# A post-norm decoder layer: P x V in two products per block, stacking by head, the last norm on VectorE, new orders

## The reference

```
Q, K = (x @ Wq.T + bq, x @ Wk.T + bk) in 16 heads of 32, each times 32**-0.25
V = x @ Wv.T + bv
x = norm(x + softmax(causal(Q K^T)) V @ Wo.T + bo)
q, k = ctx @ Wq2.T + bq2, ctx @ Wk2.T + bk2          # ctx 4 x 512 x 256, width 128
A = softmax(q k^T);  x = norm(x + x @ A^T)
xq = quantise(rms(x)), 127 steps of the row's maximum
x = norm(x + (silu(xq @ sign(Wg).T) * (xq @ sign(Wu).T)) @ sign(Wd).T)   # hidden 2048
```

## Time and profile before

| | |
|---|---|
| time, median of 3 runs (lowest, highest) | 658.28 us (655.01, 659.70) |
| the profiled execution | 660.73 us, its span 659.0 us |
| busy: TensorE, VectorE, ScalarE, GpSimd | 630.6, 496.5, 412.6, 340.8 us |
| mean granted TensorE clock | 0.983 of full speed |
| moved | 45.70 MB, 69 GB/s over the span |

### The profile page before, as it was taken

How to read it: one execution, slowest core, us unless ns; L and a number is a source line. 1 busy time by engine, 2 the same in 40 slices (tenths; PEclk the granted TensorE clock), 3 DMA queues, 4 the chain that set the end, 5 groups by cost and what they waited for, 6 DMA issues and landing times.

```text
span 659.0 us, 15461 instructions
## 1 busy us (share of the span) xinstructions
PE 630.6 (96%) x6156; PEld 445.1 (68%) x6156; DVE 496.5 (75%) x1006; ACT 412.6 (63%) x759; POOL 340.8 (52%) x472
## 2 busy tenths in 40 slices
PE   6896899999999999999999999999999999999996
PEld 5583477777666676667866766676867766586563
DVE  5764677869978977749859987866966996888764
ACT  5665799954647896434466697653456586593342
POOL 8302588514749744325477753614537743563452
PEclk9896889999999999999999999999999999999999
DMA  9696441452011011023213101031111200001000
GB/s 320 190 267 167 150 157 40 170 178 49 12 39 67 2 34 35 25 89 81 50 27 88 34 2 34 12 78 42 38 45 45 71 1 1 1 19 48 1 33 32
DMA packets 31463, 45.70 MB, mean 69 GB/s; under 512 B 5664, under 2 KB 22560, under 8 KB 29856
## 3 DMA queue, kind: packets, MB, share of 16 engines
q1 hardware_dynamic: 30848, 44.20, 22.7%
q10 hardware_dynamic: 544, 0.52, 0.2%
HBM read 27.79 MB, written 4.19 MB: 49 GB/s over the span
## 4 chain that ended last, share of the span: by engine, by line
PE 78%; DVE 10%; ACT 4%; DMA 3%; issue 3%; SPq 1%; POOL 0%; POOLq 0%; DVEq 0%; ACTq 0%
PE ps_b L657 28%; PE ps_b L840 16%; PE ps_b L825 13%; PE ps_b L752 6%; PE ps_b L733 5%; PE ps_b L761 3%; PE ps_b L714 2%; PE ps_b L710 2%; DMA hp<-in_sgT_dram 2%; PE ps_b L716 2%; DVE negm L1091 1%; SPq L619 1%; PE ps_b L670 1%; DVE bn L1027 1%; DMA st<-mrow 1%
## 5 line engine op out<-in xcount | busy, mean ns | idle before, releaser
L1284 POOL TENSOR_TENSOR ph<-p,ph 128x512 f16<-128x512 f32 x96 | 109.8, 1158 | 31.6 <-ACT ph L858 31.4
L825 PE MATMUL ps_b<-xqT,sg 128*128 128x256 f16 x1024 | 125.4, 272 | 0.1
L1280 POOL TENSOR_TENSOR hp<-gt,hp 128x512 f16<-128x512 f32 x64 | 73.9, 1160 | 87.2 <-ACT hp L858 87.0
L840 PE MATMUL ps_b<-sd,hp 128*128 128x512 fp8e4 x512 | 118.2, 379 | 0.2 <-DVE qk L1076 0.2
L1091 DVE TENSOR_REDUCE negm<-ps_b 128x1 f32<-128x512 f32 (+3 forms) x176 | 103.2, 632 | 18.4 <-PE ps_b L716 18.2
L825 PEld LDWEIGHTS ps_b<-xqT,sg 128*128 128x128 fp8e4 x1024 | 97.9, 98 | 16.6 <-DVE negm L1091 0.5
L1242 POOL TENSOR_SCALAR_AFFINE_SELECT p<-p 128x256 f32<-128x256 f32 (+1 forms) x96 | 45.7, 486 | 77.8 <-ACT p L920 76.9
L657 PE MATMUL ps_b<-xhl,wh 128*128 128x256 f16 x480 | 83.7, 273 | 0.2
L840 PEld LDWEIGHTS ps_b<-sd,hp 128*128 128x128 f16 x512 | 49.0, 98 | 51.4 <-DVE qk L1076 0.3
L1004 ACT ACTIVATE gt<-gt 128x512 f32<-128x512 f32 x64 | 40.0, 633 | 47.2 <-DVE gt L1198 47.1
L920 ACT ACTIVATE p<-ps_b 128x512 f32<-128x512 f32 x96 | 55.4, 605 | 21.5 <-PE ps_b L733 21.1
(11 more groups left out here) (133 smaller groups left out, 1218.9 us busy)
## 6 DMA issues: line engine op xcount, KB each, us to landing
st<-qk SPq DMA_DIRECT2D x192, 64.0 KB, 2.0
hp<-in_sgT_dram SPq DMA_DIRECT2D x6, 1024.0 KB, 7.1
gt<-in_sgT_dram SPq DMA_DIRECT2D x6, 1024.0 KB, 5.7
rows<-in_x_dram SPq DMA_DIRECT2D x8, 512.0 KB, 3.7
out_dram<-rows SPq DMA_DIRECT2D x16, 256.0 KB, 2.1
xin<-in_xT_dram SPq DMA_DIRECT2D x14, 256.0 KB, 3.7
e<-in_ctxT_dram SPq DMA_DIRECT2D x4, 512.0 KB, 5.6
hp<-in_wT_dram SPq DMA_DIRECT2D x4, 256.0 KB, 4.6
```

Source lines behind the costliest of these rows:

```text
L825: ins = pe.matmul(ps[:, a * HALF:(a + 1) * HALF], sg[:, ("gg", "uu").index(name), c, ht * P:(ht + 1) * P], xqT[:, c, :], start=c == 0, sto ...
L840: ins = pe.matmul(ps[:, :], hp[:, (UNITS * s + n) % HP_SLOTS, h, a, t * P:(t + 1) * P], sd[:, ht, :], start=ht == h == 0, stop=ht == HT - ...
L1280: pool.tensor_tensor(slot[:, 1, :, :], tg[:, n % 2, :, :], slot[:, 0, :, :], ALU.subtract)\
L1284: pool.tensor_tensor(out_, in_, hi, ALU.subtract).then_inc(signal, 1)
```

## The change

Four parts. (1) `weigh`: high P times [high values, ones, low values] is one product of 65 columns, low P times [high values, ones] a second of 33. Each slot of a group has 65 columns of the bank in place of 33; the eighth (t = 1, j = 3) would begin at 455 and pass column 512, so it keeps three products in 33 columns. A new step on ScalarE (`low_products`, word ov in its order) copies the low products of the seven other slots into o, and `divide` on VectorE adds them to the high ones in PSUM before reciprocal and division. o has a new layout for it. (2) A stack is now four steps of three transfers, one for each head, with a semaphore each; a maximum product waits only for the heads that it reads. (3) The norms of the last two tiles (zn3.1.0, zn3.1.1) run on VectorE; the other 14 stay on ScalarE. (4) All five orders are new texts.

```diff
--- before.py
+++ after.py
...
-lw0.0 lw0.1 lw0.2 lw0.3 lw1.0 lw1.1 lw1.2 lw1.3 lw2.0 lw2.1 lw2.2 lw2.3 lx0.1 lc0 bi lw3 sm sk0.0.0 lg0 sk0.0.1 lx1.0
...
+lw0.0 lw0.1 lw0.2 lw0.3 bi lw1.0 lw1.1 lw1.2 lw1.3 lc0 lw2.0 lw2.1 lw2.2 lw2.3 lx0.1 lg0 sm lw3 lg1 sk0.0.0.0 lg2
...
@@ -398,7 +407,7 @@
         p32 = sb("p32", [P, P32_SLOTS, S], F32)
         ph = sb("ph", [P, PH_SLOTS, 2, S], F16)
         osum = sb("osum", [P, 2, 2 * HG], F32)
-        o = sb("o", [P, T, D], F32)
+        o = sb("o", [P, 2, NG, 2, P], F32)
         rows = sb("rows", [P, T, D], F32)
         scaled = sb("scaled", [P, D], F32)
         xq = sb("xq", [P, 2, D], F16)
@@ -458,7 +467,7 @@
         r_in = [Signal(f"r_in{h}", 16) for h in range(2)]
         x_hi, x_lo = Signal("x_hi", 2), Signal("x_lo", 2)
         qk_hi, qk_lo = Signal("qk_hi", 2 * NG), Signal("qk_lo", 2 * NG)
-        stacked = [Signal(f"stacked{i}", 12 * 16) for i in range(2)]
+        stacked = [[Signal(f"stacked{i}_{j}", 3 * 16) for j in range(HG)] for i in range(2)]
         v_hi, v_lo = Signal("v_hi", 2), Signal("v_lo", 2)
         bm_red = Signal("bm_red", 1)
         m_hi, m_lo = Signal("m_hi", 2), Signal("m_lo", 2)
@@ -466,6 +475,7 @@
         p_exp, p_mask, p_hi, p_lo = Signal("p_exp", 1), Signal("p_mask", 1), Signal("p_hi", 1), Signal("p_lo", 1)
         q_exp, q_lo = Signal("q_exp", 1), Signal("q_lo", 1)
         pv_done = Signal("pv_done", NG * HG)
+        o_low, o_add = Signal("o_low", NG), Signal("o_add", NG)
         o_sum, o_out = Signal("o_sum", NG), Signal("o_out", NG)
         c_hi, c_lo = Signal("c_hi", CC), Signal("c_lo", CC)
         cq_hi, cq_lo = Signal("cq_hi", 2), Signal("cq_lo", 2)
@@ -538,6 +548,11 @@
             where = place_of(n)
             return p_lo if has_diagonal(where[0], where[2]) else q_lo, 0, among(*where) + 1
 
+        def blocks_of(ps, first, blocks, width):
+
+            whole = ps[:, :]
+            return bass.AP(whole.tensor, whole.offset + first, [whole.ap[0], [VW, blocks], [1, width]])
+
         def ph_free(eng, n):
 
             if n >= PH_SLOTS:
@@ -604,7 +619,8 @@
                 half = x[b].rearrange("(t p) d -> p t d", p=P)[:, 2 * h:2 * h + 2, :]
                 sp.dma_start(rows[:, 2 * h:2 * h + 2, :], half).then_inc(r_in[h].sem, 16)
 
-            def stack(s, gp):
+            def stack(s, gp, j):
+
                 b, h = divmod(s, 2)
                 n = 2 * s + gp
                 if n >= Q_SLOTS:
@@ -615,10 +631,9 @@
                 wait(sp, qk_lo, s, 4 * gp + 4)
                 q, k = n % Q_SLOTS, Q_SLOTS + 2 * gp + h
                 for r, (first, step) in enumerate(((0, 2), (1, 1), (0, 3))):
-                    for j in range(HG):
-                        sp.dma_start(st[DH * r:DH * (r + 1), q:k + 1:k - q, j, :, :],
-                                     qk[DH * j:DH * (j + 1), gp, first:first + step + 1:step, :, :])\
-                          .then_inc(stacked[gp].sem, 16)
+                    sp.dma_start(st[DH * r:DH * (r + 1), q:k + 1:k - q, j, :, :],
+                                 qk[DH * j:DH * (j + 1), gp, first:first + step + 1:step, :, :])\
+                      .then_inc(stacked[gp][j].sem, 16)
 
             def shift_rows(s, gp):
                 wait(sp, m_lo, s, gp + 1)
@@ -701,7 +716,8 @@
             def score_max(s, g, k):
                 h, gp, task = s % 2, g // 2, ("mx", s, g, k)
                 wait_for(pe, consts, CONSTS)
-                wait(pe, stacked[gp], s, 12 * 16)
+                for j, _, _ in MX_PIECES[h][k]:
+                    wait(pe, stacked[gp][j], s, 3 * 16)
                 ps = open_bank(task)
                 for j, qt, col in MX_PIECES[h][k]:
                     q = st[0:3 * DH, (2 * s + gp) % Q_SLOTS, j, g % 2, qt % 2 * P:(qt % 2 + 1) * P]
@@ -742,36 +758,38 @@
                     open_bank(task)
                 ps = psum[place[task][0]]
                 for t in range(2):
-                    qt, col = 2 * h + t, (HG * t + j) * (DH + 1)
+
+                    qt, col = 2 * h + t, (HG * t + j) * VW
+                    alone = col + VW > S
+                    products_of = ((0, 0, DH + 1), (0, DH + 1, DH), (1, 0, DH + 1)) if alone else ((0, 0, VW), (1, 0, DH + 1))
                     for kt in range(qt + 1):
                         k, at = p_block(h, j, kt, qt)
                         n = before(ST_PIECES, s, g, k)
                         wait(pe, *low_of(n))
-                        for half, low in ((0, 0), (0, 1), (1, 0)):
-                            part = slice(DH + 1, VW) if low else slice(0, DH + 1)
-                            ins = pe.matmul(ps[:, col:col + (DH if low else DH + 1)],
-                                            ph[:, n % PH_SLOTS, half, at:at + P], v[:, kt, HG * g + j, part],
-                                            start=kt == half == low == 0, stop=kt == qt and half == 1,
+                        for half, first, width in products_of:
+                            ins = pe.matmul(ps[:, col:col + width], ph[:, n % PH_SLOTS, half, at:at + P],
+                                            v[:, kt, HG * g + j, first:first + width],
+                                            start=kt == half == first == 0, stop=kt == qt and half == 1,
                                             skip_group_check=True)
                 ins.then_inc(pv_done.sem, 1)
 
             def flip(task, src):
                 ps = open_bank(task)
                 for c in range(C):
-                    ins = pe.transpose(ps[:, c * P:(c + 1) * P], src[:, c * P:(c + 1) * P], ident[:])
+                    ins = pe.transpose(ps[:, c * P:(c + 1) * P], src[:, c, :], ident[:])
                 done(ins, task)
 
             def flip_energies(b, t):
                 wait(pe, e_norm, b, t + 1)
-                flip(("ta", b, t), e32[:, t % 2, :])
+                flip(("ta", b, t), e32[:, t % 2, :].rearrange("p (c q) -> p c q", c=C))
 
             def flip_heads(s, t):
                 wait(pe, o_out, s, NG)
-                flip(("to", s, t), o[:, 2 * (s % 2) + t, :])
+                flip(("to", s, t), o[:, s % 2, :, t, :])
 
             def flip_rows(s, t):
                 wait(pe, o1_sum, s, t + 1)
-                flip(("tx", s, t), rows[:, 2 * (s % 2) + t, :])
+                flip(("tx", s, t), rows[:, 2 * (s % 2) + t, :].rearrange("p (c q) -> p c q", c=C))
 
             def project_context(b, i):
                 wait_for(pe, wx_lo, 1)
@@ -894,7 +912,8 @@
                 wait_for(act, bias_scaled, 2)
                 act.wait_ge(*filled("qk", s, g))
                 ps = bank_of("qk", s, g)
-                wait(act, stacked[g // 2], s, 0)
+                for signal in stacked[g // 2]:
+                    wait(act, signal, s, 0)
                 for i in range(2):
                     act.activation(qk[:, g // 2, 2 * i, g % 2, :], ps[:, i * HALF:(i + 1) * HALF], ACT.Identity,
                                    bias=bqk[:, i, g:g + 1]).then_inc(qk_hi.sem, 1)
@@ -932,6 +951,14 @@
                 ph_free(act, n)
                 act.activation(ph[:, n % PH_SLOTS, 0, :], ps[:, :], ACT.Exp, scale=EXP_SCALE)
                 act.activation(ps[:, :], ps[:, :], ACT.Exp, scale=EXP_SCALE).then_inc(q_exp.sem, 1)
+
+            def low_products(s, g):
+                wait(act, pv_done, s, HG * (g + 1))
+                if s >= 2:
+                    wait(act, to_lo, s - 1, 0)
+                mine = o[:, s % 2, g, :, :].rearrange("p t (j d) -> p (t j) d", d=DH)
+                act.activation(mine[:, 0:2 * HG - 1, :], blocks_of(bank_of("pv", s, g), DH + 1, 2 * HG - 1, DH), ACT.Copy)\
+                   .then_inc(o_low.sem, 1)
 
             def context_split(b, c):
                 wait(act, c_in, b, 16)
@@ -1014,7 +1041,7 @@
 
             in_order(ACT_ORDER, {
                 "xs": x_split, "qk": project, "va": values, "nm": maxima, "st": exponentials, "hi": p_high,
-                "sx": open_exponentials, "ez": energy_divide, "lx": load_x,
+                "sx": open_exponentials, "ov": low_products, "ez": energy_divide, "lx": load_x,
                 "n1": lambda s, t: norm(1, s, t, x2_out), "zn": lambda s, t: norm(3, s, t, z_out),
                 "cs": context_split, "cp": project_context, "en": energies, "ib": spread_steps,
                 "ta": flip_energies, "to": flip_heads, "tx": flip_rows, "tq": flip_quantised, "ga": tanh,
@@ -1105,16 +1132,17 @@
 
             def divide(s, g):
                 wait(dve, pv_done, s, HG * (g + 1))
-                if s >= 2:
-                    wait(dve, to_lo, s - 1, 0)
-                ps = bank_of("pv", s, g)[:, 0:2 * HG * (DH + 1)].rearrange("p (n d) -> p n d", d=DH + 1)
-                dve.reciprocal(osum[:, g % 2, :], ps[:, :, DH]).then_inc(o_sum.sem, 1)
+                h = s % 2
+                ps, mine = bank_of("pv", s, g), o[:, h, g, :, :].rearrange("p t (j d) -> p (t j) d", d=DH)
+                wait(dve, o_low, s, g + 1)
+                own = blocks_of(ps, 0, 2 * HG - 1, DH)
```

(18 more changed lines are left out.)

448 lines of the change are left out of this document (228 added, 220 removed).

## The result

The changed kernel takes 662.9 us in the median of its runs, the kernel before 657.2 in the median of its own on the same chips: a ratio of 1.0081, with a 95% interval of 1.0059 to 1.0102, so about 5 us slower. 644.0 was forecast, 636 to 654 as the range. The forecast was wrong, and on the wrong side. The profiled execution of the changed kernel took 663.1 us, its span 661.3; that of before had a span of 659.0.

What follows compares the result with a forecast made beforehand. TensorE, busy 630.6 of 659.0 us, was taken as the bound. The span summed as 659.0 - 11.2 (P x V) + 2.5 (new waits) - 5 (start) - 0.5 (end) = 644.8; from the median, 644 us was forecast, range 636 to 654.

Steps and rivals of the forecast that it cites:

- P x V's pace: P x V on TensorE: 65-column products at 29.4 ns, a group in 1.6 us; term -11.2 us, between -13.6 and +4.4.
- rival D: P x V: a 65-column product costs what a 128-column one does (58 ns), +4.4 for -11.2, 659.7 us; chance 0.03.
- From 88 us to the last product a microsecond taken from TensorE's own work is a microsecond of time: Middle of the kernel: TensorE's own work sets the time as long as nobody else is late.
- The new waits of the middle, +2.5 (0 to +12): New waits allowed because copy and add stand in ScalarE's and VectorE's queues: +2.5 us over the run.
- Copy and add: Each of 32 groups: copy 0.38 us, add 0.39 us, link 0.87 us, covered if ScalarE and VectorE are on time.
- rival C: Copy and add become TensorE's bound: every group shows its whole link, 27.8 us, 669.4 us in all; chance 0.05.
- The start, -5 (+3 to -9): Stacking by head and new orders: first shift rows at about 45 us, scores at 51 to 54 instead of 58.62.
- The end, -0.5: Last two norms on VectorE: no shift needed and a 0.65 us pass, -0.5 us, ends 0 and -0.8.
- Rival E: All engines' orders: the new table adds some 10 us of its own waits in the middle, about 652 us; chance 0.07.
- A: Start gains nothing, sign loads take back what shift rows gain: 649.1 us, 652 with its limit of +3; chance 0.15.

Runs made afterwards that it cites:

- bare_old: Kernel before, its orders, with P x V in two products but neither ScalarE's copy nor VectorE's add (high P times low V left out of the output): ratio 0.9940.
- new_three: Changed kernel (new orders, stacking by head, last norms on VectorE) but P x V in three products, without copy and add: 669.4 us, ratio 1.0157.
- later_old: Kernel before with two-product P x V, copy and add, VectorE's add, reciprocal and division placed 1.4 us later in its order: 15.5 us slower than pv_old.
- pv_old: Kernel before with only P x V in two products, copy on ScalarE and add on VectorE, otherwise old orders: 660.8 us, ratio 1.0034.

## Why the prediction was wrong

**P x V's pace: right.** 1.62 us for a group against 1.6 forecast, 1376 rows. TensorE's busy time is down by 9.1 us, a little less than the 10 to 12 forecast. The 65-column products start 29 ns apart in the median, so rival D is out.

**"From 88 us to the last product a microsecond taken from TensorE's own work is a microsecond of time": this step failed.** It read a busy share of 99.5% as slack on everybody else's side; its condition, "as long as nobody else is late", was booked at 2.5 us. Without copy and add, and with the orders unchanged, 11.2 us of work less gave 3.9 us of time (bare_old), and 6.3 of the rest are new waits behind 100 us (2.1 to 8.4). A timeline with 2.7 us of idle time can have another chain right under it, and no row of TensorE shows how far under. The room of the others (VectorE 402 of 512 us) is a mean and doesn't say so either.

**The new waits of the middle, +2.5 (0 to +12): this is the term that was mis-sized most, it is +11.4** by the ledger (2.1 to 13.5 behind 100 us), at the end of the range. 6.6 of it come with the new orders alone (new_three), 2.5 more when products get shorter, 2.3 with copy and add. The parts of it that have a name: the first scores of batch 1 ahead of their stacks (3.4), the energies (en2.0, 1.2), the spreading products behind quantisations beside GpSimd (1.6, 3.4, 0.7) and the slow clock behind one of them (1.7): 12.0. The energies, too, were waited for behind a quantisation in which a pass of VectorE over 128 columns took 1.05 us beside GpSimd.

**Copy and add.** As work they were sized right (0.36 and 0.39 us against 0.38 and 0.39). As a link I counted cover from one place in TensorE's order, the last step. later_old showed that a third of a further delay surfaces over the whole program, through banks held and results late. Timed, the link costs 3.9 us in the new orders and 6.2 in the old, not the 27.8 of rival C, and not nothing.

**The start, -5 (+3 to -9): wrong sign, it is about +4** in profiles that scatter by 8 us, just beyond the upper end. The step that failed: I counted SyncE's instructions ahead of the shift rows and took the rows for ready at 40.53, as before. They were ready at 48.02, since the first stacks landed late behind 1 MB loads and a sign piece stood ahead of the copy; and once issued they took 10.5 us to land, a time that the forecast of 51 to 54 for the first scores did not hold, though in the kernel before it was 8.7. The prediction named late sign pieces and full queues and gave them +3 at most. It also let 4.4 us of waits vanish with nothing in their place; waits for stacks, between 69 and 79 us and at 115 to 120, took it.

**The end, -0.5: right.** From the last product at 655.40 to the end at 661.3 are 5.9 us, against 6.35. The two norms took 0.52 and 0.55 us, not 0.65. That 0.65 was a mean of passes of 0.49 us and of some that waited for GpSimd: the mechanism that cost the middle most stood in a row that I used as a price.

**The sum** with the measured terms: 659.0 - 11.2 + 11.4 + 4 - 0.5 = 662.7 for the span, which was 661.3; by the timed ratio it is +5.3 us. Rival E had the middle right (10 us of own waits) at 0.07, and A the start at its worst end, at 0.15; no case had both, though both hang on the same new table, and together they give 658.3 - 11.2 + 10 + 3 - 0.5 = 659.6, beyond the range.

## What to carry to other kernels

Before you book a saving on the engine that is busy 99% of the time, ask what stands right under it: leave the work out without its replacement (bare_old), and see how much time goes. Where a change comes with a new order, run the old work in the new order (new_three) and the new work in the old order (pv_old) first: here one gave +10 us and the other +2, and neither was in the sum. When a transfer is on the path, ask when what it carries is ready and how long it takes to land, and not only when it can be issued. When one form of instruction has a mean well above its median, look beside what it ran before you use the mean as a price.

## What of the hardware was not expected

Passes of VectorE from SBUF to SBUF (tensor_scalar, and a scalar_tensor_tensor with two inputs there) take up to 4 times as long beside GpSimd's: 128x128 in 0.29 us in the median and up to 1.15. The long ones end 0.08 to 0.29 us behind GpSimd's pass. Passes that read PSUM kept theirs: the 64 of gt<-ps_b,invb over 512 columns all took 668 to 693 ns. A step of two elements didn't change the duration of a float32 pass over 512 columns (489 and 491 ns).

An idle time of 3.4 us on TensorE in the middle cost 1.7 us more behind it: eight 512-column products then took 3.41 us in place of 1.73, at a granted clock of 0.50.

The first two transfers of 4 KB of shift rows took 4.6 and 8.7 us to land before and 6.9 and 10.5 after, while 1 MB loads were under way; the median of all 32 after is 1.7.

Ten executions with the old order of loads differ by up to 8 us in what TensorE lost by 100 us (22.0 to 30.1), with loads of 1 MB and queues full.
